# Softmax and RMS denominators turned into 128-partition columns through DRAM before their reciprocals

## The chip, the cores and the metric

One Trainium2 chip, all 8 cores. Every core runs the same program on its own batch element, a 2048 x 1024 slice of x, and no core talks to another. The metric is the device time in microseconds of the slowest core.

## What is computed

The reference is a two-layer hybrid block: a differential cosine attention ("A"), a linear layer with int4-rounded weights and a rank-16 term ("FFN"), causal attention with rotary positions ("B"), and the FFN again, each on a layer norm and added to x. What matters here are the two attentions' denominators:

```
# attention A: 8 heads of 2 x 64; L1, L2 are cosine logits, G = tanh(gain * (L1 - L2))
A1 = softmax(L1 + G); A2 = softmax(L2 - G)
y = (A1 - lambda_full * A2) @ v
y = y * rsqrt(mean(y * y, axis=-1) + RMS_EPS) * subln_weight
# attention B: 16 heads of 64, causal
w = softmax(mask(q @ k.T / sqrt(64))); y = w @ v
```

The softmaxes are done without a running maximum: exponentials are summed, and the output is multiplied by the reciprocal of its sum afterwards.

## The kernel before

All data stands with features on partitions and the 2048 tokens along the free axis, in 4 tiles of QT = 512 tokens. The phases run one after another, with barriers at their ends. The program is written by hand as one list of operations per engine. `b.wait(engine, semaphore, value)` puts a wait into that engine's list, `b.drain` makes an engine wait for its own last operation, and `ld(G, dst, src, sem="s_gd")` (line 233) first waits until every earlier transfer on `s_gd` has landed and then issues a DMA from GpSimd's queue (POOL in the profile). The transfers of that queue are therefore strictly one after another. Every recorded operation has line 119 in the profile (the helper that replays the lists), so rows are told apart by their tiles.

**Attention A** (lines 604 to 910) runs twice (`hg`), each time over 16 instances: 4 heads by 4 token tiles. An instance is a loop of 16 steps `j` over the 128-key chunks. In a step TensorE writes two logit tiles (`a_pL`) and their difference (`a_pD`); ScalarE takes the tanh of the difference (`a_G`); VectorE adds it to one logit tile and subtracts it from the other, in place; ScalarE takes the exponential of both (`a_E`); TensorE multiplies with V into `a_pY` and sums over keys into rows 0 and 32 of `a_ps`. At the end of an instance (lines 857 to 877), the boundary, VectorE copies `a_pY` out to `a_Yr` and the two rows of sums to `rr`, takes two reciprocals of 1 x 512 on one partition each into `a_rrb`, and scales one by lambda. GpSimd writes both rows to DRAM (`scrb`) and reads them back replicated to 128 partitions (`a_rb`). VectorE uses `a_rb` after step 2 of the next instance. There the scaled outputs are subtracted (`tmpf`) and squared (`a_ysq`). In step 4 a one-column matmul sums the squares into row 0 of the PSUM tile `a_pD`; ScalarE takes the square root (`rrow`); in step 6 VectorE takes the reciprocal; GpSimd sends it through DRAM in the same way to `a_rstdb`, and VectorE uses it after step 9 (`aQ<-tmpf,a_rstdb`). ScalarE's square root is in another table than tanh and exp, so an ACT_TABLE_LOAD stands before and after it.

**Attention B** (lines 1006 to 1188) also runs twice over 16 instances: 4 pairs of heads by 4 token tiles `t_`. An instance has 4 * t_ + 4 steps: logits (`b_pS`), exponential (`b_E`), for the last four steps a triangular mask that VectorE multiplies into `b_E`, and the products with V. At its boundary VectorE copies the output to `b_Yr` and the two rows of sums to `rr`, takes two reciprocals of 1 x 512 (`b_rrb`), and GpSimd writes them as two rows and reads them back replicated (`b_rb`). VectorE waits for `b_rb` in step 1 of the next instance, writes `bQ`, and only then comes to the masks of steps 2 and later.

Of the kernel before, what the change touches and what calls it, by code (L numbers as in the profile page):

```python
# [17 lines left out]
QT = 512  # L18
# [116 lines left out]
def _ap(t, offset, dims):  # L135
    return bass.AP(t.tensor if isinstance(t, bass.AP) else t, offset, dims)
# [10 lines left out]
def build_program(n_phases=99, dbg=False):  # L147
# [4 lines left out]
    b = Builder(nc, st)  # L152
    S, V, A, P, G = b.S, b.V, b.A, b.P, b.G
# [53 lines left out]
    def sb(name, shape, dtype, stack=None):  # L207
        return (stack or st).enter_context(nc.sbuf_tensor(_u(name), list(shape), dtype))
# [18 lines left out]
    rrow = sb("rrow", (1, 1024), F32)  # L227
    sgn_col = sb("sgn_col", (128, 1), F32)
    tmpf = sb("tmpf", (128, 512), F32)
    tmpg = sb("tmpg", (128, 512), F32)  # L230
    ccol = sb("ccol", (128, 4), F32)

# [101 lines left out]
    b.inc_last("vector", "s_ve")  # L334

    a_lam = scr_alloc(32)
    b.wait("gpsimd", "s_ve")
    ld(G, d_scr[a_lam:a_lam + 1], lam_row[0:1, 0:1], sem="s_gd")
    ld(G, d_scr[a_lam + 2:a_lam + 10], srow[0:1, 272:280], sem="s_gd")
# [253 lines left out]
    if n_phases >= 0.2:  # L593
# [10 lines left out]
        for hg in range(2 if n_phases >= 0.4 else 0):  # L604
# [118 lines left out]
            rrb = sb("a_rrb", (128, QT), BF16, sc_st)  # L723
            rrow2 = rrow
            a_sc = 4 * QT * hg

            gc0 = b.cnt["s_g"]
# [16 lines left out]
            for xi, (h, t_) in enumerate(insts):  # L744
# [3 lines left out]
                for j in range(NKC):  # L748
# [45 lines left out]
                                 inc="s_g")  # L794

                    if j == 4 and prev is not None:
                        b.wait("scalar", "s_pv")
                        A.activation(rrow2[0:1, 0:QT], pD[0:1, :], AF.Sqrt,
                                     scale=1.0 / 128.0, bias=ccol[0:1, 0:1],
                                     inc="s_sq")  # L800
                        while len(sq) < xi:
                            sq.append(b.cnt["s_sq"])
                    b.wait("scalar", "s_pa", aff(pa0, jg))
                    b.wait("scalar", "s_pv", at(pv, jg - 2))
                    A.activation(Eb[sB][:, :, :], pL2[sB][:, 0:2, :], AF.Exp,
# [8 lines left out]
                    if prev is not None:  # L814
                        ph, pt = prev
                        ptsl = slice(QT * pt, QT * (pt + 1))
                        if j == 2:
                            b.wait("vector", "s_gd")
                            V.tensor_mul(y0[:], Yraw[:, 0, :], rbA[:, 0, :])
                            V.tensor_mul(tmpg[:, 0:QT], Yraw[:, 1, :], rbA[:, 1, :])  # L820
                            b.drain("vector")
                            V.tensor_sub(y0[:], y0[:], tmpg[:, 0:QT])
                            b.drain("vector")
                            V.tensor_mul(ysq[:], y0[:], y0[:])
                            b.drain("vector")
                            b.inc_last("vector", "s_ve")
                        if j == 6:
                            b.wait("vector", "s_sq", at(sq, xi - 1))
                            V.reciprocal(rrb[64:65, 0:QT], rrow2[0:1, 0:QT])
                            b.drain("vector")  # L830
                            b.inc_last("vector", "s_ve")
                            b.wait("gpsimd", "s_ve")
                            ld(G, d_scrb[a_sc + 2 * QT:a_sc + 3 * QT],
                               rrb[64:65, 0:QT], sem="s_gd")
                            b.wait("gpsimd", "s_gd")
                            ld(G, rstdb[:, :],
                               _ap(d_scrb, a_sc + 2 * QT, [[1, 1], [0, 128], [1, QT]]),
                               sem="s_gd")
                        if j == 9:
                            b.wait("vector", "s_gd")  # L840
                            V.tensor_mul(Qh[ph][:, ptsl], y0[:], rstdb[:, :])
                            b.drain("vector")
                            b.inc_last("vector", "s_ve")
# [48 lines left out]
            b.wait("scalar", "s_pv")  # L892
            A.activation(rrow2[0:1, 0:QT], pD[0:1, :], AF.Sqrt, scale=1.0 / 128.0,
                         bias=ccol[0:1, 0:1], inc="s_sq")
            b.wait("vector", "s_sq")
            V.reciprocal(rrb[64:65, 0:QT], rrow2[0:1, 0:QT])
            b.drain("vector")
            b.inc_last("vector", "s_ve")
            b.wait("gpsimd", "s_ve")
            ld(G, d_scrb[a_sc + 2 * QT:a_sc + 3 * QT], rrb[64:65, 0:QT], sem="s_gd")  # L900
# [83 lines left out]
    if n_phases >= 3:  # L984
# [21 lines left out]
        for hg in range(2):  # L1006
# [57 lines left out]
            rrbB = sb("b_rrb", (128, QT), BF16, sb_st)  # L1064
            a_sb = 2 * QT * (4 + hg)

            lm0 = b.cnt["s_lm"]
# [13 lines left out]
            for xi, (c, t_) in enumerate(instsB):  # L1081
# [78 lines left out]
                         inc="s_pv")  # L1160
                pv.append(b.cnt["s_pv"])
                b.wait("vector", "s_pv", b.cnt["s_pv"])
                V.tensor_copy(YrawB[0:64, :], pYa[0:64, :])
# [5 lines left out]
                V.reciprocal(rrbB[64:65, 0:QT], rr[64:65, 0:QT])  # L1169
                V.reciprocal(rrbB[0:1, 0:QT], rr[0:1, 0:QT])  # L1170
# [3 lines left out]
                ld(G, d_scrb[a_sb:a_sb + QT], rrbB[64:65, 0:QT], sem="s_gd")  # L1174
                ld(G, d_scrb[a_sb + QT:a_sb + 2 * QT], rrbB[0:1, 0:QT], sem="s_gd")
# [104 lines left out]
```

How the kernel before makes its waits and increments, by code:

```python
            def body(eng):  # L114
                for name, args, kw, incs in oplist:
                    if name == "wait_ge":
                        eng.wait_ge(*args)
                        continue
                    r = getattr(eng, name)(*args, **kw)
                    for s_, k_ in incs:
                        r.then_inc(sems[s_], k_)
```

## Time and profile before

| | us |
|---|---|
| median of 2 runs | 6010.93 (6006.26 to 6015.61) |
| profiled execution | 6022.94 |
| its slowest core (core 1), first to last instruction | 6021.4 |
| VectorE busy on it | 2618.3 (43%) |
| TensorE busy | 2866.1 (48%) |
| ScalarE busy | 1447.4 (24%) |
| mean granted TensorE clock | 0.627 of full speed |

No engine is busy for even half of the span: the engines wait for each other. Of the chain that ended last, VectorE has 36%, TensorE 21%, DMA 15%, the time between instructions 13% and ScalarE 12%. In the timeline a row is: start, duration, engine, operation, tile written from tiles read, how many such instructions were merged, and in brackets the idle time before it with what ended it.

### The profile page before, as it was taken

To read this page: it belongs to the slowest core of one execution; us is meant where nothing else is said; L and a number is where in the kernel's file an instruction comes from. 1 tells how busy PE (TensorE), PEld (TensorE's weight loads), DVE (VectorE), ACT (ScalarE), POOL (GpSimd) and SP (SyncE) were. 2 spreads that over 40 slices of the span, in tenths; PEclk is the share of its full clock that TensorE was granted. 3 is DMA by queue.
4 is the path that set the end of the run, shared out by engine and by line. 5 is a ranking of instruction groups with operands and counts; after the bars stand their busy time and mean duration, and the time that the engine had idled before them with its cause. 6 is when DMAs were issued, how large, how long until landed. Compare 5 with 4: busy or idle time off the path is not lost.

```text
span 6021.4 us, 35139 instructions; the slowest of 8 cores (5985.7 to 6021.4 us)
## 1 busy us (share of the span) xinstructions
PE 2866.1 (48%) x8512; PEld 694.8 (12%) x8512; DVE 2618.3 (43%) x3486; ACT 1447.4 (24%) x1528; POOL 181.6 (3%) x335
## 2 busy tenths in 40 slices
PE   0012336555555534455555555443345554556625
PEld 0000101000000011100000001111111111111201
DVE  1235334555555433355555553524544445444341
ACT  0000113444444311144444441000003320234000
POOL 0100000000000000000000000000000000000000
PEclk9995556555555555655555555676776667767758
DMA  2000000000000000000000000000100000000101
GB/s 88 26 16 7 11 17 7 6 6 6 6 6 7 6 15 14 14 6 6 6 6 6 6 6 25 9 12 4 35 21 6 6 15 21 14 6 6 29 3 68
DMA packets 102242, 86.87 MB, mean 14 GB/s; under 512 B 39038, under 2 KB 88446, under 8 KB 99742
## 3 DMA queue, kind: packets, MB, share of 16 engines
q1 hardware_dynamic: 81726, 65.43, 3.6%
q0 software_dynamic: 20320, 19.19, 1.3%
q8 instruction: 79, 1.29, 0.1%
q14 instruction: 117, 0.96, 0.1%
HBM read 73.81 MB, written 10.65 MB: 14 GB/s over the span
## 4 chain that ended last, share of the span: by engine, by line
DVE 36%; PE 21%; DMA 15%; issue 13%; ACT 12%; DVEq 2%; ACTq 0%; POOLq 0%; SPq 0%; PEldq 0%
DVE a_pL L119 8%; PE pj_p L119 7%; DVE a_rrb L119 6%; ACT a_G L119 4%; ACT a_E L119 4%; PE f_p L119 3%; DVE b_rrb L119 3%; DVE tmpf L119 3%; DMA b_rb<-scrb 2%; DMA wqb<-qout 2%; PE tm_pv L119 2%; ACT qrows L119 2%; PE b_pYb L119 2%; DMA a_rb<-scrb 2%; DMA scrb<-a_rrb 2%
## 5 line engine op out<-in xcount | busy, mean ns | idle before, releaser
L119 DVE TENSOR_TENSOR a_pL<-a_pL,a_G 128x512 f32<-128x512 f32 x1024 | 664.3, 694 | 994.2 <-ACT a_G L119 955.9
L119 PE MATMUL a_pY<-a_E,aV 128*128 128x512 bf16 x1024 | 518.4, 609 | 765.1 <-ACT a_E L119 765.1
L119 ACT ACTIVATE a_E<-a_pL,ccol 128x1024 bf16<-128x1024 f32 x512 | 570.5, 1114 | 1143.8 <-DVE a_pL L119 1143.4
L119 ACT ACTIVATE b_E<-b_pS,ccol 128x1024 bf16<-128x1024 f32 (+1 forms) x320 | 312.1, 985 | 1083.6 <-PE b_pS L119 1082.2
L119 ACT ACTIVATE a_G<-a_pD,gvec 128x512 bf16<-128x512 f32 x512 | 348.6, 681 | 87.2 <-PE a_pD L119 87.2
L119 PE MATMUL a_pD<-aQ,aKn 128*128 128x512 bf16 x512 | 307.4, 600 | 67.0 <-ACT rrow L119 49.8
L119 PE MATMUL a_pL<-aQ,aK 64*128 64x512 bf16 x1024 | 310.8, 603 | 2.9 <-DVEq L119 2.9
L119 PE MATMUL ln_px<-ln_xb,ones_col 128*1 128x512 bf16 x128 | 74.6, 583 | 495.1 <-DVEq L119 495.1
L119 PE MATMUL b_pYa<-b_E,bV 128*65 128x512 bf16 (+1 forms) x320 | 141.2, 441 | 341.2 <-DVE b_E L119 281.5
L119 PE MATMUL a_ps<-a_E,ones_col 128*1 128x512 bf16 x1024 | 302.3, 585 | 0.0
L119 ACT ACTIVATE qrows<-qrows 1x4096 bf16<-1x4096 bf16 x32 | 115.7, 3615 | 590.9 <-DVEq L119 589.4
L119 PE MATMUL pj_p<-xnA,pj_wb 128*128 128x512 bf16 x512 | 205.1, 573 | 70.3 <-DVE pj_wb L119 70.3
L119 ACT ACT_TABLE_LOAD x69 | 88.5, 1283 | 607.2 <-DVEq L119 346.6
L119 DVE RECIPROCAL b_rrb<-rr 1x512 bf16<-1x512 f32 x64 | 213.9, 3343 | 9.3 <-DVE rr L119 8.9
L119 DVE RECIPROCAL a_rrb<-rr 1x512 bf16<-1x512 f32 x64 | 213.9, 3342 | 9.0 <-DVE rr L119 8.5
L119 PE MATMUL pj_p<-bxn,pj_wb 128*128 128x512 bf16 x512 | 157.1, 462 | 121.9 <-DVE pj_wb L119 121.9
L119 PE MATMUL f_p<-fxn,f_wqb 128*128 128x512 bf16 x512 | 152.0, 450 | 114.1 <-DMA f_wqb<-wqb 57.4
L119 PEld LDWEIGHTS a_pY<-a_E,aV 128*128 128x128 bf16 x1024 | 69.7, 104 | 1007.3 <-issue 1007.3
L119 DVE TENSOR_TENSOR bQ<-b_Yr,b_rb 64x512 bf16<-64x512 f32 x64 | 43.9, 686 | 324.7 <-DMA b_rb<-scrb 324.3
L119 PE MATMUL pbcq<-qrows,ones_row 1*64 1x512 bf16 x128 | 40.5, 615 | 251.3 <-DVEq L119 251.3
L119 DVE SCALAR_TENSOR_TENSOR resid<-f_p,fb_col,resid 128x512 f32<-128x512 f32 x64 | 48.0, 750 | 240.5 <-PE f_p L119 240.5
L119 PE MATMUL b_pYb<-b_E,bV 128*64 128x512 bf16 (+1 forms) x320 | 146.3, 457 | 0.0
(144 smaller groups left out, 3067.6 us busy)
## 6 DMA issues: line engine op xcount, KB each, us to landing
resid<-xT SPq DMA_DIRECT2D x8, 1024.0 KB
qf<-fker SPq DMA_DIRECT2D x16, 512.0 KB
a_rb<-scrb POOLq DMA_DIRECT2D x32, 256.0 KB, 3.6
pj_wf<-WqkT SPq DMA_DIRECT2D x32, 256.0 KB
out<-resid SPq DMA_DIRECT2D x8, 1024.0 KB, 10.0
pj_wf<-WqT SPq DMA_DIRECT2D x16, 256.0 KB
pj_wf<-WkT SPq DMA_DIRECT2D x16, 256.0 KB
tm_wvhf<-WvT SPq DMA_DIRECT2D x16, 256.0 KB
```

The lines of the kernel that those rows point to most:

```text
L119: r = getattr(eng, name)(*args, **kw)
```

## The change

Reciprocals (and the square root) are no longer taken on rows of 1 x 512, but on columns of 128 x 4.

- A boundary and B boundary: the two rows of sums are written from `rr` to DRAM as they are (float32, 2 KB each, one after the other), read back as `xpf[:, 0:8]` (128 partitions, 2 rows, 4 values: 256 pieces of 16 bytes), and one reciprocal of 128 x 8 writes `xpb[:, 0:8]` in bf16. One DMA writes this back to `scrb` in row order (256 pieces of 8 bytes). The replicated read of `a_rb` or `b_rb` is as before.
- RMS of attention A: VectorE copies row 0 of `a_pD` to `rr` in step 4 (ScalarE took the square root there); GpSimd writes it and reads it back as 128 x 4 in step 5; ScalarE's square root of 128 x 4 is in step 6; the reciprocal of 128 x 4 in step 7; the write-back (128 pieces of 8 bytes) and the replicated read in step 8. The use stays in step 9.
- The same after the last instance of each half of A, without steps between.
- VectorE waits for `s_gd` ahead of each new use of `rr`.

The core of the diff (a line of "..." where lines are left out):

```diff
+    xpf = sb("xpf", (128, 12), F32)
+    xpb = sb("xpb", (128, 12), BF16)
...
                     if j == 4 and prev is not None:
-                        b.wait("scalar", "s_pv")
-                        A.activation(rrow2[0:1, 0:QT], pD[0:1, :], AF.Sqrt,
-                                     scale=1.0 / 128.0, bias=ccol[0:1, 0:1],
-                                     inc="s_sq")
+                        b.wait("vector", "s_pv", b.cnt["s_pv"])
+                        b.wait("vector", "s_gd")
+                        V.tensor_copy(rr[0:1, 0:QT], pD[0:1, :])
+                        b.drain("vector")
+                        b.inc_last("vector", "s_sq")
...
+                    if j == 5 and prev is not None:
+                        b.wait("gpsimd", "s_sq", at(sq, xi - 1))
+                        ld(G, d_scr[a_tp + 2 * QT:a_tp + 3 * QT], rr[0:1, 0:QT],
+                           sem="s_gd")
+                        b.wait("gpsimd", "s_gd")
+                        ld(G, xpf[:, 8:12],
+                           _ap(d_scr, a_tp + 2 * QT, [[4, 128], [1, 4]]),
+                           sem="s_gd")
+                    if j == 6 and prev is not None:
+                        b.wait("scalar", "s_gd")
+                        A.activation(xpf[:, 8:12], xpf[:, 8:12], AF.Sqrt,
+                                     scale=1.0 / 128.0, bias=ccol[:, 0:1],
+                                     inc="s_se")
+                    if j == 7 and prev is not None:
+                        b.wait("vector", "s_se")
+                        b.wait("vector", "s_gd")
+                        V.reciprocal(xpb[:, 8:12], xpf[:, 8:12])
...
+                    if j == 8 and prev is not None:
+                        b.wait("gpsimd", "s_ve")
+                        ld(G, _ap(d_scrb, a_sc + 2 * QT, [[4, 128], [1, 4]]),
+                           xpb[:, 8:12], sem="s_gd")
+                        b.wait("gpsimd", "s_gd")
+                        ld(G, rstdb[:, :],
+                           _ap(d_scrb, a_sc + 2 * QT, [[1, 1], [0, 128], [1, QT]]),
+                           sem="s_gd")
...
-                        if j == 6:
-                            b.wait("vector", "s_sq", at(sq, xi - 1))
-                            V.reciprocal(rrb[64:65, 0:QT], rrow2[0:1, 0:QT])
...
                 b.inc_last("vector", "s_ev")
-                V.reciprocal(rrb[0:1, 0:QT], rr[0:1, 0:QT])
-                V.reciprocal(rrb[32:33, 0:QT], rr[32:33, 0:QT])
+                b.wait("gpsimd", "s_ev")
+                ld(G, d_scr[a_tp:a_tp + QT], rr[0:1, 0:QT], sem="s_gd")
+                ld(G, d_scr[a_tp + QT:a_tp + 2 * QT], rr[32:33, 0:QT], sem="s_gd")
+                b.wait("gpsimd", "s_gd")
+                ld(G, xpf[:, 0:8],
+                   _ap(d_scr, a_tp, [[4, 128], [QT, 2], [1, 4]]), sem="s_gd")
+                b.wait("vector", "s_gd")
+                V.reciprocal(xpb[:, 0:8], xpf[:, 0:8])
                 b.drain("vector")
-                V.tensor_scalar_mul(rrb[32:33, 0:QT], rrb[32:33, 0:QT],
-                                    lam_col[32:33, 0:1])
+                V.tensor_scalar_mul(xpb[:, 4:8], xpb[:, 4:8], lam_col[:, 0:1])
                 b.drain("vector")
                 b.inc_last("vector", "s_ve")
                 b.wait("gpsimd", "s_ve")
-                ld(G, d_scrb[a_sc:a_sc + QT], rrb[0:1, 0:QT], sem="s_gd")
-                ld(G, d_scrb[a_sc + QT:a_sc + 2 * QT], rrb[32:33, 0:QT], sem="s_gd")
+                ld(G, _ap(d_scrb, a_sc, [[4, 128], [QT, 2], [1, 4]]),
+                   xpb[:, 0:8], sem="s_gd")
                 b.wait("gpsimd", "s_gd")
```

B's boundary is changed in the same way, with rows 64 and 0 of `rr` and no lambda.

## Rows read from the trace of the kernel before

**Rows 1.** Waits of the whole span: who waited for whom, us, times, longest
```profile
PE b_pYa L119 <- DVE b_E L119: 281.5, 64, 12.4
```

**Rows 2.** Timeline of VectorE at a boundary of attention A
```profile
1143.83 1.36 DVE L119 COPY rr<-a_ps 1x512 f32<-1x512 f32 x2
1145.46 6.70 DVE L119 RECIPROCAL a_rrb<-rr 1x512 bf16<-1x512 f32 x2 [0.27 <-DVE rr L119]
1152.27 0.34 DVE L119 TENSOR_SCALAR a_rrb<-a_rrb,lam_col 1x512 bf16<-1x512 bf16 x1
1153.01 1.30 DVE L119 TENSOR_TENSOR a_pL<-a_pL,a_G 128x512 f32<-128x512 f32 x2 [0.41 <-DVE a_rrb L119]
...
1159.63 1.30 DVE L119 TENSOR_TENSOR a_pL<-a_pL,a_G 128x512 f32<-128x512 f32 x2 [2.01 <-ACT a_G L119]
```

**Rows 3.** Timeline of GpSimd's queue at the same boundary
```profile
1153.37 0.49 POOL L119 DMA_DIRECT2D scrb<-a_rrb  x1 [38.48 <-DVEq L119]
...
1157.62 0.56 POOL L119 DMA_DIRECT2D a_rb<-scrb  x1 [1.67 <-DMA scrb<-a_rrb]
```

**Rows 4.** DMA issues of the span: count, KB each, median us from issue to landing
```profile
a_rb<-scrb POOLq DMA_DIRECT2D x32, 256.0 KB, 3.6
...
a_rstdb<-scrb POOLq DMA_DIRECT2D x32, 128.0 KB, 3.4
...
b_rb<-scrb POOLq DMA_DIRECT2D x32, 128.0 KB, 5.0
...
wqb<-qout POOLq DMA_DIRECT2D x64, 32.0 KB, 1.7
scrb<-a_rrb POOLq DMA_DIRECT2D x96, 1.0 KB, 1.6
...
am_col<-scr POOLq DMA_DIRECT2D x2, 0.5 KB, 3.2
```

**Rows 5.** Who waited for a_rb on core 1: us in total, times
```profile
  DVE tmpf L119: 31.0, 28
```

**Rows 6.** Timeline of VectorE: a reciprocal of one element
```profile
127.65 0.15 DVE L119 RECIPROCAL srow<-srow 1x1 f32<-1x1 f32 x1
```

**Rows 7.** Timeline of ScalarE in step 4 of an instance of A
```profile
1098.25 1.28 ACT L119 ACT_TABLE_LOAD   x1 [2.40 <-PE a_ps L119]
...
1101.54 1.11 ACT L119 ACTIVATE a_E<-a_pL,ccol 128x1024 bf16<-128x1024 f32 x1
```

**Rows 8.** Timeline of VectorE in steps 6 and 7 of that instance
```profile
1106.71 1.30 DVE L119 TENSOR_TENSOR a_pL<-a_pL,a_G 128x512 f32<-128x512 f32 x2 [2.01 <-ACT a_G L119]
1108.05 3.34 DVE L119 RECIPROCAL a_rrb<-rrow 1x512 bf16<-1x512 f32 x1
1111.79 1.30 DVE L119 TENSOR_TENSOR a_pL<-a_pL,a_G 128x512 f32<-128x512 f32 x2 [0.41 <-PE a_pL L119]
```

**Rows 9.** Chains in time order, start-up: cores 0, 1, then twice core 3
```profile
105.91 7.91 DMA scr<-am_col
...
109.08 15.39 DMA scr<-am_col
...
104.81 11.59 DMA qf<-fker
...
118.77 7.61 DMA scr<-am_col
```

**Rows 10.** Timeline of VectorE over one instance of attention B
```profile
4559.08 0.68 DVE L119 COPY rr<-b_pYb 1x512 f32<-1x512 f32 x1
...
4576.93 1.38 DVE L119 TENSOR_TENSOR bQ<-b_Yr,b_rb 64x512 bf16<-64x512 f32 x2 [10.21 <-DMA b_rb<-scrb]
4579.09 0.36 DVE L119 TENSOR_TENSOR b_E<-b_E,tri_bf 128x128 bf16<-128x128 bf16 x2 [0.77 <-ACT b_E L119]
```

**Rows 11.** Busy time by stretch (attention A, then B), granted clock, DMA share, GB/s
```profile
1000.00:1840.00 840.00, 488.80 (x1303) 80.02 (x1303) 433.45 (x524) 353.55 (x407) 31.31 (x60) 0.51 0.03 6
...
4500.00:4940.00 440.00, 240.32 (x796) 65.73 (x797) 194.57 (x254) 152.97 (x156) 28.74 (x48) 0.67 0.03 8
```

More of the change, by code:

```diff
@@ L336, in build_program @@
     a_lam = scr_alloc(32)
+    a_tp = scr_alloc(3 * 512)
     b.wait("gpsimd", "s_ve")
@@ L722, in build_program @@
             rstdb = sb("a_rstdb", (128, QT), BF16, sc_st)
-            rrb = sb("a_rrb", (128, QT), BF16, sc_st)
-            rrow2 = rrow
             a_sc = 4 * QT * hg
@@ L796, in build_program @@
                     if j == 4 and prev is not None:
-                        b.wait("scalar", "s_pv")
-                        A.activation(rrow2[0:1, 0:QT], pD[0:1, :], AF.Sqrt,
-                                     scale=1.0 / 128.0, bias=ccol[0:1, 0:1],
-                                     inc="s_sq")
+                        b.wait("vector", "s_pv", b.cnt["s_pv"])
[3 more added lines that the diff above has]
+                        b.inc_last("vector", "s_sq")
                         while len(sq) < xi:
                             sq.append(b.cnt["s_sq"])
+                    if j == 5 and prev is not None:
[15 more added lines that the diff above has]
+                        V.reciprocal(xpb[:, 8:12], xpf[:, 8:12])
+                        b.drain("vector")
+                        b.inc_last("vector", "s_ve")
+                    if j == 8 and prev is not None:
[6 more added lines that the diff above has]
+                           sem="s_gd")
                     b.wait("scalar", "s_pa", aff(pa0, jg))
@@ L826, in build_program @@
                             b.inc_last("vector", "s_ve")
-                        if j == 6:
-                            b.wait("vector", "s_sq", at(sq, xi - 1))
-                            V.reciprocal(rrb[64:65, 0:QT], rrow2[0:1, 0:QT])
[L830 to L838, printed above, removed]
                         if j == 9:
@@ L863, in build_program @@
                 b.inc_last("vector", "s_ev")
-                V.reciprocal(rrb[0:1, 0:QT], rr[0:1, 0:QT])
-                V.reciprocal(rrb[32:33, 0:QT], rr[32:33, 0:QT])
+                b.wait("gpsimd", "s_ev")
[4 more added lines that the diff above has]
+                   _ap(d_scr, a_tp, [[4, 128], [QT, 2], [1, 4]]), sem="s_gd")
+                b.wait("vector", "s_gd")
+                V.reciprocal(xpb[:, 0:8], xpf[:, 0:8])
                 b.drain("vector")
-                V.tensor_scalar_mul(rrb[32:33, 0:QT], rrb[32:33, 0:QT],
-                                    lam_col[32:33, 0:1])
+                V.tensor_scalar_mul(xpb[:, 4:8], xpb[:, 4:8], lam_col[:, 0:1])
                 b.drain("vector")
@@ L891, in build_program @@
                      tile_position=(0, 0), inc="s_pv")
[L892 to L896, printed above, removed]
+            b.wait("vector", "s_pv", b.cnt["s_pv"])
+            b.wait("vector", "s_gd")
+            V.tensor_copy(rr[0:1, 0:QT], pD[0:1, :])
             b.drain("vector")
@@ L899, in build_program @@
             b.wait("gpsimd", "s_ve")
-            ld(G, d_scrb[a_sc + 2 * QT:a_sc + 3 * QT], rrb[64:65, 0:QT], sem="s_gd")
+            ld(G, d_scr[a_tp + 2 * QT:a_tp + 3 * QT], rr[0:1, 0:QT], sem="s_gd")
+            b.wait("gpsimd", "s_gd")
+            ld(G, xpf[:, 8:12], _ap(d_scr, a_tp + 2 * QT, [[4, 128], [1, 4]]),
+               sem="s_gd")
+            b.wait("scalar", "s_gd")
+            A.activation(xpf[:, 8:12], xpf[:, 8:12], AF.Sqrt, scale=1.0 / 128.0,
+                         bias=ccol[:, 0:1], inc="s_se")
+            b.wait("vector", "s_se")
+            V.reciprocal(xpb[:, 8:12], xpf[:, 8:12])
+            b.drain("vector")
+            b.inc_last("vector", "s_ve")
+            b.wait("gpsimd", "s_ve")
+            ld(G, _ap(d_scrb, a_sc + 2 * QT, [[4, 128], [1, 4]]), xpb[:, 8:12],
+               sem="s_gd")
             b.wait("gpsimd", "s_gd")
@@ L1063, in build_program @@
             rbB = sb("b_rb", (128, QT), BF16, sb_st)
-            rrbB = sb("b_rrb", (128, QT), BF16, sb_st)
             a_sb = 2 * QT * (4 + hg)
@@ L1162, in build_program @@
                 b.wait("vector", "s_pv", b.cnt["s_pv"])
+                b.wait("vector", "s_gd")
                 V.tensor_copy(YrawB[0:64, :], pYa[0:64, :])
@@ L1168, in build_program @@
                 b.inc_last("vector", "s_ev")
-                V.reciprocal(rrbB[64:65, 0:QT], rr[64:65, 0:QT])
-                V.reciprocal(rrbB[0:1, 0:QT], rr[0:1, 0:QT])
+                b.wait("gpsimd", "s_ev")
+                ld(G, d_scr[a_tp:a_tp + QT], rr[64:65, 0:QT], sem="s_gd")
+                ld(G, d_scr[a_tp + QT:a_tp + 2 * QT], rr[0:1, 0:QT], sem="s_gd")
+                b.wait("gpsimd", "s_gd")
+                ld(G, xpf[:, 0:8],
+                   _ap(d_scr, a_tp, [[4, 128], [QT, 2], [1, 4]]), sem="s_gd")
+                b.wait("vector", "s_gd")
+                V.reciprocal(xpb[:, 0:8], xpf[:, 0:8])
                 b.drain("vector")
@@ L1173, in build_program @@
                 b.wait("gpsimd", "s_ve")
-                ld(G, d_scrb[a_sb:a_sb + QT], rrbB[64:65, 0:QT], sem="s_gd")
-                ld(G, d_scrb[a_sb + QT:a_sb + 2 * QT], rrbB[0:1, 0:QT], sem="s_gd")
+                ld(G, _ap(d_scrb, a_sb, [[4, 128], [QT, 2], [1, 4]]),
+                   xpb[:, 0:8], sem="s_gd")
                 b.wait("gpsimd", "s_gd")
```

## The prediction

> **What bounds the kernel now.** I read the busy shares and the chain of waits first. No engine is busy for half of the span, so only places where one engine holds the others count. TensorE waits 281.5 us for VectorE's masks in attention B [rows 1]. In attention A the loop turns once in 3.31 us through VectorE, ScalarE and back, and everything placed between two adds of VectorE beyond its idle 2.01 us is paid in full [rows 8]. The two timelines of a boundary [rows 2, 10] then show what each change touches. GpSimd's queue and the landing times [rows 3, 4] price the DMAs. The granted clock is about half of full speed in A, and 0.67 in B [rows 11]: A is at 1.2 GHz nearly all the time and can lose little there.
>
> **A's boundary.** The sums are in `rr` at 1145.19, and the first add of the next instance starts at 1153.01, 7.82 us later [rows 2]. Removed are 6.70 us of reciprocals and the scaling of 0.34. What comes in their place is a wait of VectorE for three DMAs, one after another. From VectorE's last result to the first DMA issue pass 0.76 us (1152.61 to 1153.37) [rows 2, 3]. Two row writes take 4.25 us until the next issue [rows 3]. The read of 256 pieces of 16 bytes is not in this trace. The nearest row is the read of 128 pieces of 4 bytes, 3.2 us. I take that; the ends are 1.7 (the cheapest 128-piece DMA) and 5.0 (the dearest read) [rows 4]. Then come two small operations of 0.15 [rows 6] with gaps, and the 0.41 before the add, 0.86 in all. Sum 0.76 + 4.25 + 3.2 + 0.86 = 9.07. The boundary gets 1.25 us longer, not shorter. Queued behind VectorE's wait are the adds of the next instance, and behind those ScalarE's exponentials and TensorE's products.
>
> **The write-back, the term that decides.** `xpb` goes back as 256 pieces of 8 bytes into 2 KB of DRAM; call its time to landing W. At the boundary it replaces two row writes. The trace holds one DMA of the kind: at start-up 128 pieces of 4 bytes go from a column to 512 neighbouring bytes. It took 7.61 us on core 3 and 15.39 on core 1, the least and the most of eight, one per core. On core 1 it began while the same write of core 0 (7.91) was in flight, and a 512 KB load on core 3 took 11.59 us in these microseconds [rows 9]. A write of 128 pieces of 256 bytes lands in 1.7, a whole row in 1.6 [rows 4]. So it isn't the number of pieces but their smallness: 7.61 - 1.6 = 6.0 us for 128, or 47 ns each. Two things differ from the new write-back: it has twice as many pieces (W = 1.6 + 256 x 0.047 = 13.6 if each piece costs the same), and each is twice as large and the whole four times as spread (W = 4.6 if pieces only hinder each other within the same stretch of memory, half as many per stretch). Nothing here tells these apart. I take 8.6 for W, between them, close to the least measured and with a little for meetings of two cores; and 7.6 for the RMS write-back W' of 128 pieces. Both ends stay for the range, and 1.6, no penalty at all, as a rival.
>
> The Trainium skill (DMA: Bandwidth & Descriptors, Specifications) says that a transfer under 512 bytes is done as a read-modify-write; by that rule the 256-byte pieces ought to suffer too, and their 1.7 us [rows 4] does not show it. The same page's Anatomy of one DMA fits a GpSimd DMA as about 2.0 us plus bytes over 436 GB/s; the write-back would then be about 2.0, an estimate from the page, and the total would be that of the second rival below. The start-up write [rows 9] speaks against it.
>
> **Step 2 of A.** With the first add at a0, the write-back is issued at a0 + 0.36, as the first row write is now [rows 2, 3]. A landing to the next issue is 4.25 / 2 - 1.6 = 0.52, and the replicated read takes 3.6 [rows 3, 4]. So `a_rb` lands at a0 + 4.5 + W. VectorE wants it at a0 + 7.9, after the third add [rows 2]. It waits W - 3.4 = 5.2 us where it now waits 31.0 us in 30 instances [rows 5], 1.0 each: +4.2. The next add waits for VectorE directly, so all of it counts.
>
> **Steps 4 to 9 of A.** Now ScalarE starts its table load at 1098.25, released by a matmul, and the exponential starts 3.29 us later at 1101.54: two loads of 1.28 and the root [rows 7]. Then VectorE copies the row at that moment (0.68, as in [rows 10]), waits about 0.4 and adds for 1.30; the exponential starts at about 1100.8: -0.75. In step 6 ScalarE does two loads of 1.28 and a root of 128 x 4, taken as 0.2, before an exponential that would start about 1.6 us after the tanh (the two adds, 1.30, and a handover on either side): 2.8 - 1.6 = +1.2. The row write and the column read, issued at 1099.7, land 2.12 + 3.2 later at 1105.0, just before the tanh of step 6 ends; at a read of 5.0 ScalarE waits 1.1 more. In step 7 the reciprocal of 3.34 goes: adds of steps 6 and 7 start 1106.71 and 1111.79, 5.08 apart instead of 3.31 [rows 8], so -1.77; its successor of 0.15 fits into VectorE's idle time. The `a_rstdb` chain (0.76 + W' + 0.52 + 3.4) starts at about 1107.5 and is wanted at 1118.4 less the gains, with 1.3 us of idle beyond; W' = 7.6 costs 0.2. If that cover were gone, each further us of W' would cost one. Sum: -0.75 + 1.2 - 1.77 + 0.2 = -1.1.
>
> **A in all.** 1.25 + 4.2 - 1.1 = +4.4 us for 30 instances: +132. The last instance of each half has nothing to hide in: up to `a_rb` 0.76 + 4.25 + 3.2 + 0.45 + 0.76 + W + 0.52 + 3.6 = 13.5 + W = 22.1 against 16.0 now (1145.19 to 1157.62 + 3.6) [rows 2 to 4]; the RMS chain adds a row write and a column read (5.3) and the longer write-back (6.0) and drops 3.34 and 0.5 of root: +7.5. Two halves: 2 x 13.6 = +27.
>
> **B's boundary.** From the last copy (4559.76) to the product with `b_rb` (4576.93) pass 17.17 us [rows 10]. New: 0.76 + 4.25 + 3.2 + 0.2 for the column and its reciprocal, 0.76 + W + 0.52 + 5.0 for the way back: 14.7 + W = 23.3, that is +6.1. VectorE stands at this wait with the masks behind it, and TensorE with its products behind those. In every kind of instance the masks follow at once; only in that with 12 steps before its first mask does VectorE then wait for ScalarE, 0.77 us, 0.43 more than its least gap [rows 10]. 32 boundaries, 8 of them with this slack of 0.4: 32 x 6.1 - 3 = +192.
>
> **Sum.** 132 + 27 + 192 = +351 us on the profiled execution's 6022.9 (span 6021.4): 6374. That execution stands 12.0 us above the median of the runs, so 6362 in their terms, +5.8%. One more microsecond of W costs 30 + 2 + 32 = 64 us.
>
> **Rivals.**
> 1. *Each small piece costs the same.* W = 13.6, W' = 7.6: +5.0 x 64 = 320 more: 6680. For it: 47 ns each on a core that wrote alone, and that the writes of neighbouring cores hinder each other and a large load, so that a shared resource is held. Against: the new pieces are spread over four times the bytes.
> 2. *Small pieces are free here; no change* (the other side). W = W' = 1.6: `a_rb` is no longer waited for, A's inner instances get 1.25 - 1.0 - 1.3 = -1.1 each (-32), the tails 2 x (-0.9 + 1.5) = +1, B 32 x (16.3 - 17.17) = -28: about 5952, -1.0%. The start-up write would have to be slow for a reason of its own. It decides only below W = 2.5, where B's chain is no longer than now. A gain above 2% isn't there even then: the reciprocals that go are replaced on VectorE's path by DMAs just as long.
> 3. *Pieces hinder each other only within a stretch.* W = W' = 4.6: A 30 x (1.25 + 0.2 - 1.3) = +5, tails 2 x (2.1 + 4.5) = +13, B 32 x 2.1 = +67: 6096, +1.4%. For it: eight-byte pieces fill a stretch with half as many.
>
> **How the numbers follow.** The forecast (W from 6 to 11) gets 0.42, rival 1 or a still longer W through meetings of cores 0.24, rival 3 0.24, rival 2 0.08, and 0.02 for something unseen that gains. 2%, about what a measurement can tell, is 120 us or W = 5.1. The forecast and rival 1 lie above, and so does 0.04 of rival 3, with a dearer column read (1.8 us more on 64 boundaries is 115 us): slower 0.70. Within 2% 0.28, faster 0.02. Range 6080 to 6720: from rival 3 to rival 1, with 0.1 left out on either side.
>
> **What would show it.** The landing time of `scrb<-xpb`, of 256 and of 128 pieces: 8.6 and 7.6. `xpf<-scr` at 3.2. VectorE's gap between the copies to `rr` and the next add at 9.1. VectorE idle before `tmpf<-a_Yr,a_rb` about 5 us. The adds of steps 6 and 7 3.3 us apart plus the 1.2 of table loads. From B's last copy to `bQ` 23 us. If `scrb<-xpb` lands in 2 us, the forecast is wrong by some 400 us; a column read of 5 adds 115. If in B the longer stalls push the granted clock down from 0.67, it is too low.

## The result and the profile after

Where no two neighbouring cores end late together, the changed kernel takes a little longer than the kernel before: those executions against those of before give a ratio of 1.0169 (95% interval 1.0144 to 1.0193), within the 2% that count as no change. That number can't be understood without the rest: of its 11 timed runs (6095.8 to 6465.1 us, where the kernel before stays between 6005.3 and 6016.7) the seven long ones are those in which one or more pairs of neighbouring cores end late together, and the ratio leaves them out. The median of all eleven, 6234.8, is 3.7% above that of before, 6010.1. The forecast was 6362, with 6080 to 6720 as range and "slower" at 0.70. Three of the long runs, at 6339.0 and 6354.8 (twice), end near the forecast; that is no hit, since they are long by late pairs and not by the term that was to make the time.

The profiled execution shows both kinds of core side by side. Spans and mean granted clocks by core:

```profile
core 2: 6337.4 us, clock 0.620
core 3: 6336.5 us, clock 0.621
core 4: 6046.0 us, clock 0.626
core 5: 6096.3 us, clock 0.627
```

Cores 2 and 3 end within 1 us of each other and 240 us after core 5. I read the result on cores 4 and 5, which stayed free of this, and come back to the pair below.

**Where the time goes on core 5.** It was 6003.7 us before and is 6096.3 now, +93. From the first `tmpf<-a_Yr,a_rb` to the last `aQ<-tmpf,a_rstdb`, all of attention A but its first instance, it took 2687.9 us and takes 2727.6, +40; from B's first to its last `bQ` 1079.5 and now 1131.5, +52. On core 4 the two are +10 and +48, on core 2 +161 and +156.

VectorE at a boundary of A, core 5 (start, duration, operation, merged count, idle before it); it answers to [rows 2]:

```profile
1149.66 1.37 DVE L119 COPY rr<-a_ps 1x512 f32<-1x512 f32 x2
1158.46 0.20 DVE L119 RECIPROCAL xpb<-xpf 128x8 bf16<-128x8 f32 x1 [7.43 <-DMA xpf<-scr]
1158.78 0.23 DVE L119 TENSOR_SCALAR xpb<-xpb,lam_col 128x4 bf16<-128x4 bf16 x1
1159.41 1.29 DVE L119 TENSOR_TENSOR a_pL<-a_pL,a_G 128x512 f32<-128x512 f32 x2 [0.41 <-DVE xpb L119]
```

6.70 us of reciprocals have become 0.20, and in their place VectorE idles 7.43. From the end of the copies to the first add pass 8.38 us, where it was 7.82. GpSimd's queue at the same place says why; it answers to [rows 3]:

```profile
1151.80 0.51 POOL L119 DMA_DIRECT2D scr<-rr  x1 [31.44 <-DVEq L119]
1153.93 0.50 POOL L119 DMA_DIRECT2D scr<-rr  x1 [1.61 <-DMA scr<-rr]
1156.12 0.75 POOL L119 DMA_DIRECT2D xpf<-scr  x1 [1.69 <-DMA scr<-rr]
1159.81 0.73 POOL L119 DMA_DIRECT2D scrb<-xpb  x1 [2.94 <-DVEq L119]
1164.48 0.56 POOL L119 DMA_DIRECT2D a_rb<-scrb  x1 [3.94 <-DMA scrb<-xpb]
```

Five transfers stand in a row where three stood. The landing times (size, median us) on core 5, then on core 2; they answer to [rows 4]:

```profile
a_rb<-scrb POOLq DMA_DIRECT2D x32, 256.0 KB, 4.3
...
b_rb<-scrb POOLq DMA_DIRECT2D x32, 128.0 KB, 5.4
...
xpf<-scr POOLq DMA_DIRECT2D x64, 4.0 KB, 2.1
scrb<-xpb POOLq DMA_DIRECT2D x64, 2.0 KB, 4.1
...
scrb<-xpb POOLq DMA_DIRECT2D x32, 1.0 KB, 3.7
```

```profile
b_rb<-scrb POOLq DMA_DIRECT2D x32, 128.0 KB, 7.1
...
scrb<-xpb POOLq DMA_DIRECT2D x64, 2.0 KB, 3.7
```

The write-back lands in 4.1 us on core 5 (3.6 on core 4), not in 8.6. On core 2 the median of all is no worse, but single write-backs take up to 9.9 us where on core 4 none takes more than 4.2, and the replicated read after it went from 5.0 us [rows 4] to 7.1.

### The profile page after: what moved, and what is told of

Same layout as the page of the kernel before. It is cut to its first block, busy times and chain, and to the rows that moved or that the text cites. A ratio compares the mean times of both kernels' runs of the same rounds, so it can differ in the third digit from the quotient of the medians.

```text
span 6337.4 us, 36001 instructions; the slowest of 8 cores (6037.8 to 6337.4 us)
## 1 busy us (share of the span) xinstructions
PE 2866.2 (45%) x8512; PEld 691.7 (11%) x8512; DVE 2117.7 (33%) x3454; ACT 1433.9 (23%) x1528; POOL 314.8 (5%) x527
## 4 chain that ended last, share of the span: by engine, by line
DMA 28%; DVE 27%; PE 19%; issue 13%; ACT 10%; DVEq 2%; ACTq 0%; POOLq 0%; SPq 0%; PEldq 0%
DVE a_pL L119 7%; DMA scrb<-xpb 7%; PE pj_p L119 6%; DMA b_rb<-scrb 4%; ACT a_G L119 4%; DMA scr<-rr 4%; ACT a_E L119 3%; DVE tmpf L119 3%; DMA a_rb<-scrb 3%; PE f_p L119 3%; DMA xpf<-scr 2%; DMA a_rstdb<-scrb 2%; PE tm_pv L119 2%; DMA wqb<-qout 2%; ACT qrows L119 2%
## 5 line engine op out<-in xcount | busy, mean ns | idle before, releaser
L119 POOL DMA_DIRECT2D scr<-rr x160 | 81.9, 512 | 4237.7 <-DVEq L119 4115.8
L119 DVE RECIPROCAL xpb<-xpf 128x8 bf16<-128x8 f32 x96 | 18.7, 194 | 519.7 <-DMA xpf<-scr 491.1
L119 PE MATMUL b_pS<-bQ,bK 64*128 64x512 bf16 (+3 forms) x640 | 137.0, 445 | 4.7 <-DVEq L119 4.7
```

Of the source, the lines that this page charges most:

```text
L119: r = getattr(eng, name)(*args, **kw)
```

## The experiments

**The theory.** The change trades VectorE's long reciprocals for DMAs in the same chain. What it costs is the landing time of the small-piece write-back, paid at nearly every boundary, and that time is 3 to 4 us for a core alone, and longer, along with the replicated read, when the neighbouring core's small pieces are in flight. **Rivals:** the late pairs come from the clock, whatever the kernel writes; or it is the number of pieces, or the added transfers as such, and not the pieces' smallness.

**The parts one by one.** Each kernel keeps one part of the change and has the code of before for the others.

```diff
# a_only: kept at A's boundary; rms_only: kept in steps 4 to 8; b_only: kept at B's boundary
-                V.reciprocal(rrb[0:1, 0:QT], rr[0:1, 0:QT])
-                V.reciprocal(rrb[32:33, 0:QT], rr[32:33, 0:QT])
+                ld(G, d_scr[a_tp:a_tp + QT], rr[0:1, 0:QT], sem="s_gd")
+                ld(G, d_scr[a_tp + QT:a_tp + 2 * QT], rr[32:33, 0:QT], sem="s_gd")
...
```

> Only A's boundary goes through columns (row writes, column read, write-back of 256 pieces of 8 bytes); the RMS chain and B are as before. Theory (each DMA pays its place in the chain, and the write-back of small pieces lands in about 4 us when alone and in more when the other core of a pair writes at the same time): the boundary gets 0.6 us longer and the wait for a_rb about 1 us longer, 1.6 x 32 = +50 us, so about 6060, with more on single executions whose two neighbouring cores (0 and 1, 2 and 3, ...) write together; the two cores of such a pair then end together. Rival (the long executions of the changed kernel come from the chip's clock, whatever the kernel writes): no pair of cores stands out from the others beyond what the kernel before shows (30 us).

Measured: median 6164.9 us (6040.2 to 6172.1) against 6002.1. By core:

```profile
core 4: 5986.3 us, clock 0.633
core 5: 6036.9 us, clock 0.627
core 6: 6164.5 us, clock 0.627
core 7: 6170.5 us, clock 0.627
```

Cores 6 and 7 end 130 us after core 5 at the same granted clock, 0.627. The clock isn't the cause of this. Landing times, of `a_rb` on core 6 and of `scrb<-xpb` on core 7:

```profile
DMA to landing us min/median/max: 5.1/9.0/9.9
```

```profile
DMA to landing us min/median/max: 5.9/7.4/8.5
```

On core 4 `scrb<-xpb` lands in 3.0 / 3.5 / 4.0. On core 7 not one of the 32 write-backs lands in less than 5.9 us, and on core 6 not one replicated read in less than 5.1. Cores 2 and 3 (6081.8 and 6096.1) show both cases one after the other: in the first half of A the reads of core 2 land in a median of 8.9 us and the write-backs of core 3 in 7.3, in the second half in 3.6 and 3.9. So this is no mishap now and then: it lasts for a whole half of A, or for both.

This reading has two limits. Each core's times are counted from its own first instruction, so no trace shows transfers of two cores in flight at once; that they meet is inferred from slow transfers on both cores of a pair. And core 6's own write-backs (median 3.4) aren't slow, so it stays open whether core 7's are held by them or by core 6's replicated reads.

The theory's direction holds; its +50 was right for a core like 5 (about +40), too much for core 4 (none), and too little for a pair that meets.

> Only the RMS chain goes through columns (128 pieces of 8 bytes); both boundaries are as before. Theory: the wait in step 4 gets 0.7 us shorter, the root in step 6 costs 1.3 and the reciprocal of 1.77 goes, -1.1 us in 30 instances, +2 us at each of two tails: about -29 us, 5982. The write-back is hidden up to W' = 7.4, so collisions of neighbouring cores cost nothing here. Rival (the write-back is paid): at or above the kernel before.

Measured: 6057.6 us (6029.1 to 6069.5) against 6002.1, ratio 1.0081 (1.0051 to 1.0110). The number was missed by 76 us, and it lies where the rival had it. In the profile cores 2, 3, 6 and 7 end between 5955.9 and 5970.1, which is about the expected gain; cores 4 and 5 end at 5989.8 and 5979.1, cores 0 and 1 at 6015.4 and 6027.6. VectorE's wait for `a_rstdb` (total, times), core 0, then core 6:

```profile
  DVE aQ L119: 68.7, 18
```

```profile
  DVE aQ L119: 16.9, 3
```

On core 0 the write-back takes up to 8.0 us and the read after it up to 10.5, on core 6 up to 3.7 and 3.9. The theory had counted on cover for the write-back alone. So even a small-piece write that is hidden while a core is alone has its price.

> Only B's boundary goes through columns. Theory: from the last copy to the product with b_rb 18.7 us instead of 17.2, all of it paid, 32 x 1.5 = +48 us, 6058 where neighbouring cores do not collide, and more where they do, because the chain has no slack and both the write-back and the read of b_rb are in it. Rival (TensorE's clock, lowered by longer stalls, makes the loss): the granted clock of the B stretch is lower than before and the DMAs are not longer.

Measured: 6091.7 us (6028.0 to 6121.0) against 6002.1, ratio 1.0109 (1.0025 to 1.0194). In the profile core 4 ends at 5996.9, core 5 at 6023.2, cores 0 and 1 at 6068.5 and 6064.1. On core 0 VectorE waits 364.6 us for `b_rb`, on core 4 312.9, and GpSimd waits 146.4 us for the write-back against 104.9. Together that is 93 us, more than the 72 by which core 0 ends later. The granted clock of the stretch from 4500 to 5600 us is lower too, 0.66 and 0.67 on cores 0 and 1 against 0.69 on core 4. So half of what the rival asked for is seen, a lower clock, but not its other half, transfers of the same length; the longer transfers suffice for the loss.

**Same bytes, larger pieces.** The columns are made of fewer partitions; nothing else changes.

```diff
-                ld(G, _ap(d_scrb, a_sc, [[4, 128], [QT, 2], [1, 4]]), xpb[:, 0:8], sem="s_gd")
+                ld(G, _ap(d_scrb, a_sc, [[32, 16], [QT, 2], [1, 32]]), xpb[0:16, 0:64], sem="s_gd")
# wide64: [[8, 64], [QT, 2], [1, 8]] and xpb[0:64, 0:16]; both also for xpf, B and the RMS chain
```

> As the changed kernel, but the columns are 16 partitions x 32 values instead of 128 x 4: the write-backs have 32 (and 16) pieces of 64 bytes, the column reads as many of 128 bytes; the same bytes in all. Theory (the smallness of the pieces costs): the write-back lands in 1.6 to 1.9 us, a_rb is no longer waited for, B's chain is 16.6 us; A (0.6 - 1.0 - 1.1) x 30 = -45, B -0.6 x 32 = -19, so about 5950, and no execution has a pair of cores far above the others. Rival (any DMA of many partitions to DRAM costs 4 us, or the added transfers themselves collide): about the time of the changed kernel, 6100 to 6400, with the same spread.

Measured: 5942.0 us (5939.6 to 5946.2) against 6002.1, ratio 0.9896 (0.9881 to 0.9911). Landings on core 0:

```profile
xpf<-scr POOLq DMA_DIRECT2D x64, 4.0 KB, 1.8
scrb<-xpb POOLq DMA_DIRECT2D x64, 2.0 KB, 1.6
```

The cores end between 5907 and 5945, and the runs lie 7 us apart, not 370. The number of transfers, their bytes and their order are those of the changed kernel; only the pieces differ. So the pieces are the cause of both the time and its spread. Their size, their number and the count of partitions change together here, and in the column read as well as in the write-back; the next two runs take size, number and partitions apart for a core's own landing times. Whether it is the small write or the small column read that holds a neighbour, none of the runs tells for certain. VectorE over one boundary of B, core 5:

```profile
4605.27 0.68 DVE L119 COPY rr<-b_pYb 1x512 f32<-1x512 f32 x1
4613.34 0.54 DVE L119 RECIPROCAL xpb<-xpf 16x64 bf16<-16x64 f32 x1 [7.39 <-DMA xpf<-scr]
4622.04 1.39 DVE L119 TENSOR_TENSOR bQ<-b_Yr,b_rb 64x512 bf16<-64x512 f32 x2 [8.16 <-DMA b_rb<-scrb]
```

From the last copy to `bQ` 16.1 us; before it was 17.2 [rows 10], in the changed kernel 18.7 (4623.31 to 4642.01 on core 5).

> As the changed kernel, with columns of 64 partitions x 8 values: write-backs of 128 (and 64) pieces of 16 bytes, column reads as many pieces of 32 bytes. Theory (only neighbours below 16 bytes hinder each other; the number of pieces is free): the write-back lands in 1.7 us, the time is that of 16 partitions, about 5945, and no pair of cores stands out. Rival (the gain of the 16-partition form came from its few pieces or few partitions): between that and the changed kernel, 6000 to 6100, with pairs that stand out.

Measured: 5976.5 us (5950.9 to 6020.9) against 6010.7, ratio 0.9951 (0.9915 to 0.9986). Neither side had the time: it lies between the theory's 5945 and the rival's 6000 to 6100. Landings on core 2:

```profile
b_rb<-scrb POOLq DMA_DIRECT2D x32, 128.0 KB, 6.4
...
scrb<-xpb POOLq DMA_DIRECT2D x64, 2.0 KB, 1.8
```

For a core alone the theory is right: 16-byte pieces land in a median of 1.8 us, and six of the eight cores end between 5904 and 5927, as all do with 16 partitions (5907 to 5945). So 64 partitions and 128 pieces do as well as 16 and 32; that it wasn't the halving from 256 pieces to 128 either, the next run shows. It is wrong on the pairs: cores 2 and 3 end at 5967.4 and 5965.9, and on core 2 `b_rb` takes 6.4 us in the median where core 4 has 4.8. So pieces of 16 bytes (32 in the column read) cost a core alone nothing and still come with late pairs; those of 64 bytes (128 in the column read) did neither.

**The pieces by themselves.** Of the kernel only the start-up and the output are left; neither attention nor FFN is computed.

```diff
+    kinds = [("w4", 128, 1, 1), ("w8", 128, 2, 2), ("w16", 128, 4, 4), ("w32", 128, 8, 8), ("w64", 128, 16, 16),
+             ("w128", 128, 32, 32), ("w8far64", 128, 2, 16), ("w8far256", 128, 2, 64), ("w8of16", 16, 2, 2), ("w4b", 128, 1, 1)]
...
+        for r in range(4):
+            ld(G, _ap(d_scr, a0, [[pitch, parts], [1, w]]), t[0:parts, 0:w], sem="s_gd")
```

> Only the start-up and the output are left of the kernel (neither attention nor FFN is computed; out is x), and after the start-up GpSimd writes columns to DRAM, four times each, one after another: 128 pieces of 4, 8, 16, 32, 64 and 128 bytes side by side, 8 bytes at a pitch of 64 and of 256 bytes, 16 pieces of 8 bytes, and the 256 pieces of 8 bytes of the changed kernel. Theory 1 (small pieces hinder each other when they fall into the same 64 bytes): 4 bytes are dearest (6 to 8 us), 8 bytes 3 to 4, 64 bytes and more 1.6 to 1.8, and 8 bytes at a pitch of 64 as cheap as 64-byte pieces. Theory 2 (each partial piece costs the same, wherever it falls): 4, 8 and 16 bytes equal, 256 pieces twice 128, and the pitch changes nothing. Theory 3 (the start-up write of 7.6 us was slow for what ran beside it, the 512 KB loads): 4-byte pieces here cost no more than 8-byte ones, 3 to 4 us.

DMA issues of core 0 (128 pieces each, so 0.5 KB are pieces of 4 bytes, 1 KB of 8, 2 KB of 16; `p_w8far` the pieces apart, `p_w8of` 16 pieces, `p_two` 256 pieces; medians of four):

```profile
scr<-p_w8far POOLq DMA_DIRECT2D x8, 1.0 KB, 1.7
scr<-p_w POOLq DMA_DIRECT2D x4, 0.5 KB, 16.4
scr<-p_w POOLq DMA_DIRECT2D x4, 1.0 KB, 4.1
scr<-p_w POOLq DMA_DIRECT2D x4, 2.0 KB, 1.7
scr<-p_w POOLq DMA_DIRECT2D x4, 4.0 KB, 1.7
...
scr<-p_w8of POOLq DMA_DIRECT2D x4, 0.1 KB, 1.8
scr<-p_w4b POOLq DMA_DIRECT2D x4, 0.5 KB, 8.0
scrb<-p_two POOLq DMA_DIRECT2D x4, 2.0 KB, 3.6
```

Theory 1 holds in kind, though not in its 64 bytes. Eight bytes with room around them cost 1.7 us, side by side 4.1; 256 pieces cost no more than 128, though 16 cost only 1.8; from 16 bytes on, also side by side, there is no price. Theory 2 falls with the pitch and with the 256 pieces, theory 3 with the 4-byte pieces, which are slow with nothing beside them on their own core: 8.0 in the last series, 16.4 in the first. The 16.4 is twice what was expected. On cores 2 to 7 the 8-byte pieces take 5.5 to 6.7 us in the median, and the 4-byte pieces of the last series 10.6 to 13.3 on cores 1 to 7. All cores write in this kernel, so I read the least of the eight medians, 8.0 and 4.1, as nearest to a core alone, and take the rest to be the neighbour's; that is argued, since no run had one core write alone.

> The changed kernel with the write-back at both boundaries issued twice, one after the other. Each adds landing and next issue, 3.4 to 3.9 + 0.7 us. By the sum of the forecast a microsecond there costs 64 us (30 inner instances and 2 tails of A, 32 boundaries of B), so 4.3 x 64 = +275 over the changed kernel where cores do not collide: 6370 against 6096, and more collisions. Rival (part of the way back is hidden, in A behind the three adds, in B behind products that have other work): +100 to +180.

```diff
                 ld(G, _ap(d_scrb, a_sc, [[4, 128], [QT, 2], [1, 4]]), xpb[:, 0:8], sem="s_gd")
+                ld(G, _ap(d_scrb, a_sc, [[4, 128], [QT, 2], [1, 4]]), xpb[:, 0:8], sem="s_gd")
```

Measured: 6957.8 us (6827.5 to 7001.2) against 6010.7, ratio 1.1431 (1.1343 to 1.1520), 590 us more than expected. Neither side had it. On core 4 of the profiled execution:

```profile
DVE bQ L119 <- DMA b_rb<-scrb: 723.8, 32, 23.6
...
DVE tmpf L119 <- DMA a_rb<-scrb: 494.8, 32, 23.4
```

On core 4 of the changed kernel these waits were 324.0 and 34.2. One more write-back should add 4.3 us each time and added 12.5 in B and 14.4 in A, since `a_rb` now lands in 9.7 us in the median (3.6) and the write-backs in 6.5 (3.5), at most 9.8. In that execution all eight cores end late, between 6776.4 and 6999.6. In the three others some pairs do escape for the most part: the earliest pair of each ends at 6369.4 and 6422.6, 6352.1 and 6407.0, 6356.5 and 6446.8. Of two such cores the faster ends 310 to 340 us after its like in the changed kernel (6033 to 6046), where the theory had +275 without meetings and the rival +100 to +180. So the rival is out: a microsecond on this path is paid nearly everywhere, and the rest up to 6958 comes with late pairs. A second estimate is the comparison of wide16 with the changed kernel: 2.5 us less write-back and 0.3 less read (4.1 to 1.6, 2.1 to 1.8), and 154 us less (5942.0 against 6095.8), 55 us for each; it is rough, as the RMS write-back changes with them. The forecast's sum had 64.

> The changed kernel once more, for a profile beside those of the other kernels. Theory (collisions of neighbouring cores): where both cores of a pair end more than 60 us late, both, and only they, show replicated reads or write-backs with medians of 5 us or more; cores that end near 6040 show write-backs of 3.0 to 3.8 us. Rival (the clock): late pairs show the same transfers and a lower granted clock in the same stretches.

Measured: 6264.1 us in one execution. Cores 0 and 1 end at 6238.0 and 6262.5, the others between 5994.0 and 6060.8. Landings on core 0:

```profile
a_rb<-scrb POOLq DMA_DIRECT2D x32, 256.0 KB, 5.8
...
b_rb<-scrb POOLq DMA_DIRECT2D x32, 128.0 KB, 5.0
...
scrb<-xpb POOLq DMA_DIRECT2D x32, 1.0 KB, 6.4
```

Cores 0 and 1 have `a_rb` at 5.8 and 5.6 us in the median and the RMS write-back at 6.4, where cores 2 to 7 have 3.6 to 4.0 and 3.1 to 3.6. For these two transfers the theory's line at 5 us divides the cores rightly. For `b_rb` it doesn't, since that read lands in 4.9 to 5.2 on all cores, late or not: this pair was late by A alone. The granted clock between 1000 and 1840 us, in A, is 0.50 to 0.51 on all of them.

**Without the detour.** One instruction over all partitions between the two rows takes both reciprocals, in the kernel before:

```diff
-                V.reciprocal(rrb[0:1, 0:QT], rr[0:1, 0:QT])
-                V.reciprocal(rrb[32:33, 0:QT], rr[32:33, 0:QT])
+                V.reciprocal(rrb[0:33, 0:QT], rr[0:33, 0:QT])
```

> The kernel before, with the two reciprocals of a boundary as one over all partitions between the two rows (33 in A, 65 in B; the rows between hold ones or old values and are not used). If a reciprocal's time goes by the values of one partition, as theory has it, one costs 3.34 us, the boundary of A is 3.36 us shorter (-107 us), and B's chain 13.8 us instead of 17.2, of which the instances with 12 steps before the first mask gain nothing (24 x 3.35 = -80): about 5820. Rival (it goes by all values): no gain or a loss.

Measured: 5817.3 us (5816.1 to 5827.9) against 5998.7, ratio 0.9698 (0.9683 to 0.9712), as expected to 3 us. The groups of VectorE:

```profile
L119 DVE RECIPROCAL b_rrb<-rr 65x512 bf16<-65x512 f32 x32 | 107.2, 3349 | 8.5 <-DVE rr L119 8.5
L119 DVE RECIPROCAL a_rrb<-rr 33x512 bf16<-33x512 f32 x32 | 107.0, 3344 | 8.5 <-DVE rr L119 8.5
```

33 or 65 partitions take what one takes. Attention A gets 107 us shorter on core 1 and B 83, which are the two parts of the sum.

```diff
# best: the reciprocal, the scaling and the DMAs stand behind the first add of the next instance (j == 0);
# the use of a_rb in step 3 instead of 2; two rows in one write; b_rb replicated to 128 partitions
+                ld(G, _ap(d_scrb, a_sc, [[QT, 2], [1, QT]]), rrb[0:64:32, 0:QT], sem="s_gd")
+                ld(G, rbB[:, :, :], _ap(d_scrb, a_sb, [[1, 1], [0, 128], [1, 2 * QT]]), sem="s_gd")
# best2: best, and the RMS chain of the change with columns of 16 partitions
```

> As merged, and in A the reciprocal stands behind the first add of the next instance, the use of a_rb after its fourth add; the two rows go to DRAM in one DMA; b_rb is read as one row replicated to 128 partitions (twice the bytes). Theory: A's boundary from copy to add about 0.5 us instead of 7.8, the reciprocal costs 2.1 us beyond VectorE's idle time, 32 x -5.3 = -170 us; B's chain 0.3 + 3.3 + 0.8 + 2.1 + 3.6 = 10.1 us instead of 17.2, paid in full in the instances with 0 and 4 steps before the first mask (16 x 7) and in part in the others (some 30): in all -310, about 5700. Rival (VectorE's own work now bounds A): less than 100 us in A.

Measured: 5647.9 us (5640.7 to 5658.3), ratio 0.9412 (0.9396 to 0.9428). VectorE at A's boundary, core 1:

```profile
1063.71 1.36 DVE L119 COPY rr<-a_ps 1x512 f32<-1x512 f32 x2
1065.48 1.30 DVE L119 TENSOR_TENSOR a_pL<-a_pL,a_G 128x512 f32<-128x512 f32 x2 [0.41 <-DVE rr L119]
1066.81 3.35 DVE L119 RECIPROCAL a_rrb<-rr 33x512 bf16<-33x512 f32 x1
```

The add follows the copies at once, and the reciprocal works while ScalarE does. The expected time, about 5700, was missed by 52 us on the good side. On core 1 A is 180 us shorter than before (the expectation had 170) and B 163 (it had 140). In B nothing was moved: what B gained beyond the 83 us of merged comes with one row write fewer and with the read of `b_rb`, which is twice as large here and lands sooner:

```profile
b_rb<-scrb POOLq DMA_DIRECT2D x32, 256.0 KB, 3.5
```

Before, two halves of 64 partitions each took 5.0 us for 128 KB [rows 4].

> The kernel with the merged and moved reciprocal, and the RMS chain through columns of 16 partitions x 32 values. Theory: the RMS part alone is worth -1.1 us in 30 instances (-33) and costs about 2 us at each of two tails, as its write-back of 64-byte pieces is hidden: 5648 - 29 = about 5620. Rival (with a_rb now used after the fourth add, the copy of the row in step 4 and the waits for GpSimd's queue come too close and stall VectorE): no change or slower than 5648.

Measured: 5624.6 us (5617.4 to 5631.6) against 6010.7, ratio 0.9356 (0.9342 to 0.9370), as expected to 5 us. The RMS part of the change was worth 20 to 30 us, with larger pieces; the intervals of best and best2 don't overlap.

## Why the prediction was wrong

The step that failed is the size of the write-back, "the term that decides". I took 8.6 us for 256 pieces of 8 bytes, from a write of 128 pieces of 4 bytes that took 7.6 [rows 9]. It lands in 3.4 to 4.2 on cores that do not meet, and the RMS write-back, W' = 7.6, in 3.1 to 3.7. The two ends I had set were 13.6 and 4.6, and I chose between them, near the measured row, where the row was of another kind: the cost is not in a piece but in neighbours that are too small. 8 bytes for 4 takes it from 8.0 to 4.1, 16 to 1.7, and twice the pieces add nothing. At 64 us for each microsecond, 4.4 to 5.2 too much is some 280 to 330 us, more than the whole miss against the four runs without late pairs (6095.8 to 6141.6). The trace of before could not tell the ends apart, and no row of it spoke for 8.6 rather than 4.6. That core 3 wrote alone was itself an assumption, since the times of two cores aren't counted from the same moment.

Rival 3, hindrance within a stretch, had the mechanism nearly right and the number, 6096, partly by luck: its W of 4.6 is above the 3.4 to 4.2 measured, it shares the column read that was 1.1 us too dear, and against these stand a longer wait for `a_rb` on core 5 and dearer tails than it had. Of its +85 us it put 18 into A and 67 into B, where core 5 shows 40 and 52.

The Trainium skill's rule that under 512 bytes a transfer is a read-modify-write (DMA: Bandwidth & Descriptors, Specifications) does not by itself tell the dear pieces from the cheap ones: those of 16 to 128 bytes landed in 1.7 us here. The fit of the same page of the Trainium skill, 2.0 us plus bytes (Anatomy of one DMA), is near those 1.7 us; 4.1 us for 8 bytes is twice and 8.0 us for 4 bytes four times what it gives.

The other terms, in the prediction's order:

- **A's boundary**, +1.25 expected, +0.56 measured (8.38 against 7.82). Right in sign and mechanism; the column read lands in 2.1 us and not 3.2, the two small operations take 0.20 and 0.23 and not 0.15 each.
- **Step 2**, +4.2 expected. The waits for `a_rb` are 71.4 us in 32 on core 5 against 32.8, and 34.2 against 32.6 on core 4. In each of these sums the two tails have some 8.5 us apiece before and 8.7 to 11.4 after. Inside the instances the wait is thus 1.7 us where it was 0.5 on core 5, +1.1, and 0.6 where it was 0.5 on core 4. The same slip is in the forecast: of the 31.0 us on core 1 [rows 5] 17.5 are the tails', and 0.5 us, not 1.0, are left for each of the 30 instances. The formula W - 3.4 was right; with W at 4.1 and `a_rb` landing in 4.3 us and not in 3.6 it gives 1.4 on core 5. W was not.
- **Steps 4 to 9**, -1.1 expected. In step 4 two adds are 6.72 us apart where it was 7.38; in steps 6 and 7 4.62 where it was 5.08 [rows 8]: -1.12. ScalarE's root of 128 x 4 takes 0.30 between its two loads of 1.28. `a_rstdb` is in time.
- **A's two tails**, +13.6 each expected. On core 4 the second gets 0.4 us longer up to `a_rb` and 7.3 in the RMS chain, on core 5 3.3 and 8.6 (its write-back there took 6.3). The expected 7.5 for the RMS chain thus came out with a write-back half as long, by luck: GpSimd's queue idles 4.6 us between the row write and the column read, for nothing that the profile shows, where in the steps it waits 1.7. The sum had no such term, and its cause is open. On core 5, 30 x (0.56 + 1.1 - 1.12) = 16 and two such tails, 24, make the +40 that A as a whole measured.
- **B's boundary**, +6.1 expected, +1.5 measured (18.70 against 17.17). The same W; all of it is paid, as foreseen: 32 x 1.5 = 48 of the 52 us on core 5.
- **Meetings of cores** stood in one half-sentence as "a little" and as part of rival 1's chance. They are worth more than everything else: in the changed kernel a pair that meets ends from some 110 to more than 370 us later. That they may occur was in [rows 9]; that a pair, once together, stays together for whole phases, I did not foresee. That it holds itself so (the later core is delayed behind the earlier, and both then run the same distance to the next boundary) is argued from a_only's 32 of 32 and from its cores 2 and 3, which parted between the halves of A; it is not shown by an experiment of its own.
- **The clock** stayed at 0.50 in A, the lower of its two levels, and moved by about 0.01 in the mean; in the stretch from 4500 to 5600 us it was 0.67 to 0.68 after and 0.68 to 0.70 before. In b_only it was 0.66 and 0.67 on the late pair against 0.69, where the longer transfers suffice for the loss. No run shows a part for it beyond that.

## What to carry to other kernels

Time on a long one-partition operation isn't won by sending the row through DRAM into columns: in a dependent chain each DMA costs about 2.2 us with its issue, and three of them kept VectorE waiting 7.4 us where two reciprocals of 512 values took 6.7. Look first for the same operation on more partitions at once, which was free here and gave 3.0%, and for a place behind the next step's critical instruction; together with one row write fewer and a replicated read in another form they gave 5.9%, with no transfer added. If a column must go to DRAM, give each piece 64 bytes, the least here that cost neither a core alone nor its neighbour, and time a kernel of several cores over many runs: a cost that one core doesn't have alone shows in the spread before it shows in the median.

## What the runs showed of the hardware

- Writes of 128 pieces side by side, GpSimd's queue, least of the eight cores' medians: 8.0 us at 4 bytes, 4.1 at 8, 1.7 from 16 bytes on (probe); 8 bytes at a pitch of 64 or 256 bytes 1.7; 16 pieces of 8 bytes 1.6; 256 pieces of 8 bytes 3.3. Reads of 256 pieces of 16 bytes take 2.1 (after). The pitch from which pieces of 8 bytes no longer hinder each other is above 8 and at most 64 bytes and was not measured closer.
- Neighbouring cores (0 and 1, 2 and 3, 4 and 5, 6 and 7) slow each other while small pieces are in flight, by inference from pairs that are slow together: in a_only the write-backs of core 7 land in 7.4 us where core 4's take 3.5, and the replicated reads of 256 KB of core 6 in 9.0 where core 4's take 3.6. In double, with twice as many write-backs at the boundaries, all four pairs were slow in the profiled execution. With pieces of 64 bytes (wide16) no pair stood out in four executions.
- A reciprocal of 512 values takes 3.34 to 3.35 us on 1, 33 or 65 partitions (before, merged).
- A replicated read as one row over 128 partitions, 256 KB, lands in 3.5 us (best); as two rows over 64 partitions each, 128 KB, it takes 5.0 (before).
